# A stack of four graph layers on one core: products of zeros behind each group's sums on TensorE

## What is computed

```python
edge_index = jnp.stack([src, dst])
h = relu(layernorm(x)); x = x + L0(h)   # GAT: scores from 2 vectors, softmax over each target's edges
h = relu(layernorm(x)); x = x + L1(h)   # relational: a row of h @ W[type] for each edge, summed at dst
h = relu(layernorm(x)); x = x + L2(h)   # two GCN convolutions: rows summed at dst, twice
h = relu(layernorm(x)); x = x + L3(h)   # two transformer convolutions, 4 heads, softmax over edges
...
def _transformer_conv(x, src, dst, ea, Wq, bq, Wk, bk, Wv, bv, We, Ws, bs, H, C):
    ...
    alpha = jnp.einsum('ehc,ehc->eh', q[dst], kj) / jnp.sqrt(jnp.asarray(C, x.dtype))
    amax = jax.ops.segment_max(alpha, dst, num_segments=n)
    p = jnp.exp(alpha - amax[dst])
    denom = jax.ops.segment_sum(p, dst, num_segments=n)
    w = p / denom[dst]
    msg = (vj * w[..., None]).reshape(-1, H * C)
    out = jax.ops.segment_sum(msg, dst, num_segments=n)
    return out + x @ Ws + bs
```

## Time and profile before

| | before |
|---|---|
| three runs | 4387.75 us median (4380.13 to 4401.72) |
| profiled execution | 4389.91 us, span 4387.9 us |
| granted TensorE clock, mean | 0.772 |
| busy, share of the span | PE 64%, PEld 46%, DVE 47%, ACT 35%, POOL 54% |
| products (PE) | 15364 |
| DVE's 104 additions, first to last start: L0 | 253.9 to 883.8 us |
| the same: L1 | 985.5 to 1566.9 us |
| the same: L2, first and second | 1649.9 to 2158.3, 2209.9 to 2727.2 us |
| the same: L3, first and second | 2921.3 to 3545.6, 3706.9 to 4347.7 us |

### The profile page before, as it was taken

How to read it: one execution, slowest core, us unless ns; L and a number is a source line. 1 busy time by engine, 2 the same in 40 slices (tenths; PEclk the granted TensorE clock), 3 DMA queues, 4 the chain that set the end, 5 groups by cost and what they waited for, 6 DMA issues and landing times.

```text
span 4387.9 us, 52346 instructions
## 1 busy us (share of the span) xinstructions
PE 2793.6 (64%) x15364; PEld 2036.7 (46%) x15364; DVE 2080.7 (47%) x4427; ACT 1555.9 (35%) x3919; POOL 2371.9 (54%) x2449
## 2 busy tenths in 40 slices
PE   3177788872333356877767877557676774666667
PEld 2055556632222334555534554345555553455555
DVE  5033334641222345566546655235555663555557
ACT  2054444540000033333343333234454423444443
POOL 1745555116666636666366664335666534555653
PEclk9976666885555668899879988567888886887887
DMA  4322222131111112222122221345555424455541
GB/s 86 68 56 59 62 60 62 23 130 47 46 46 48 45 56 53 53 53 53 53 61 55 53 52 34 105 126 141 139 144 146 129 81 128 135 139 135 146 135 45
DMA packets 351656, 360.74 MB, mean 82 GB/s; under 512 B 125198, under 2 KB 274389, under 8 KB 351381
## 3 DMA queue, kind: packets, MB, share of 16 engines
q0 software_dynamic: 89600, 211.77, 18.4%
q1 hardware_dynamic: 255638, 143.69, 12.7%
q10 hardware_dynamic: 6148, 1.93, 0.3%
HBM read 327.08 MB, written 30.26 MB: 81 GB/s over the span
## 4 chain that ended last, share of the span: by engine, by line
PE 41%; another core or an unknown queue 21%; DVE 15%; issue 15%; ACT 3%; POOL 1%; DMA 1%; SPq 1%; DVEq 1%; ACTq 1%; POOLq 0%
PE QX L1368 20%; PE NU L1368 12%; PE MTB L1368 7%; DVE sums_transposed L834 3%; DVE extra_sums_transposed L834 2%; DVE gathered_rows L834 1%; DVE messages L834 1%; DVE query_key_products L834 1%; POOL gathered_rows L549 1%; PE MID L1368 1%; SPq L436 1%; DVE scan_scores L981 1%; ACT window_distance L698 1%; ACTq L601 0%
## 5 line engine op out<-in xcount | busy, mean ns | idle before, releaser
L532 POOL DMA_INDIRECT gathered_rows<-key_value_rows,src_index x832 | 829.6, 997 | 646.2 <-DVE messages L834 356.3
L834 DVE TENSOR_TENSOR sums_transposed<-sums_transposed,NU 128x512 f32 x624 | 425.7, 682 | 1140.7 <-remote 740.6
L549 POOL DMA_INDIRECT gathered_rows<-gcn_rows,src_index x720 | 684.5, 951 | 470.0 <-issue 194.6
L532 POOL DMA_INDIRECT gathered_rows<-gat_rows,src_index x416 | 397.0, 954 | 391.6 <-DVE messages L1008 191.1
L1368 PE MATMUL NU<-start_penalty,zero_weights 128*128 128x512 bf16 x624 | 278.5, 446 | 423.1 <-DVE sums_transposed L834 328.1
L549 POOL DMA_INDIRECT gathered_rows<-relation_rows,src_relation_index x416 | 400.9, 964 | 206.2 <-issue 123.8
L794 ACT ACTIVATE gathered_rows<-iota_window,dst_in_window_by_edge 128x128 f32<-128x128 f32 x832 | 265.1, 389 | 608.4 <-remote 445.0
L729 ACT ACTIVATE edge_node_onehot<-iota_window,dst_in_window_by_edge 128x128 f32<-128x128 f32 x1248 | 394.8, 387 | 155.1 <-remote 135.4
L1368 PEld LDWEIGHTS NU<-edge_node_onehot,messages 128*128 128x128 f32 x2496 | 414.0, 234 | 47.0 <-issue 26.5
L1368 PE MATMUL NU<-gathered_rows 128*128 128x128 f32 x2496 | 395.5, 310 | 56.5 <-issue 33.3
L1368 PE MATMUL NU<-edge_node_onehot,messages 128*128 128x128 f32 x2496 | 413.6, 318 | 24.7 <-issue 24.6
(11 more groups left out here) (294 smaller groups left out, 4357.0 us busy)
## 6 DMA issues: line engine op xcount, KB each, us to landing
query_window<-query_rows SPq DMA_DIRECT2D x832, 66.0 KB
dst_in_window_row<-dst_in_window SPq DMA_DIRECT2D x156, 256.0 KB
gathered_rows<-key_value_rows,src_index POOLq DMA_INDIRECT x832
relation_rows<-gathered_rows SPq DMA_DIRECT2D x25, 512.0 KB
gathered_rows<-gcn_rows,src_index POOLq DMA_INDIRECT x720
dst_in_window_row<-src_place_and_block SPq DMA_DIRECT2D x28, 256.0 KB
gathered_rows<-gat_rows,src_index POOLq DMA_INDIRECT x416
query_window<-gat_target_scores SPq DMA_DIRECT2D x416, 2.0 KB
```

Source lines behind the costliest of these rows:

```text
L532: pool.indirect_dma_start(out=rows_of(a, s)[:, t, :], out_offset=None, in_=a["table"], in_offset=bass.IndirectOffsetOnAxis(ap=srcI[:, TPG ...
L549: pool.indirect_dma_start(out=linear_rows(p["k"], k)[:, t, :], out_offset=None, in_=p["table"], in_offset=bass.IndirectOffsetOnAxis(ap=p[" ...
L834: return dve.tensor_tensor(o, x, y, op)
```

## The change

Behind the sums of a group TensorE now issues the clear of the next group's bank, and ahead of that clear the same product of zeros several times more. Each writes zeros into the bank that is about to be cleared, so nobody reads them. In the attention passes `stay_busy(s)` does it at the end of steps 2 to 114: 14 products in each of the steps 2 to 10, in which no sums run yet, then five and the clear up to step 103, then the clear alone. In `linear` it is 14 and the clear in the relation pass, four and the clear in the GCN passes, and the clear alone behind a pick. In all, 3591 products of zeros are added. The clear of NU leaves `node_sums`, where it had stood behind the wait for the messages; its new wait is for DVE's addition of two groups before (`nu_used`).

```diff
+    FILLING, SUMMING, BETWEEN = 14, 6, (15, 5, 5)
...
+            def keep_busy(bank, n):
+                for _ in range(n):
+                    mm(bank[:, 0:SPAN], zeros_w[:], fpen[:, 0:TPG, :].rearrange("q c p -> q (c p)"))
...
                     pe.wait_ge(S["msg_ready"], b + s + 1)
-                    clear(NU[s % 2], P)
                     for t in range(TPG):
...
+                def stay_busy(s):
+                    g = s + 1 - LAG
+                    if s == 2:
+                        if L3:
+                            pe.wait_ge(S["fin_used"], NBK * (2 + k))
+                        else:
+                            pe.wait_ge(S["idx_ready"], 2)
+                    if g >= 2:
+                        pe.wait_ge(S["nu_used"], b + g - 1)
+                    if g < 0:
+                        keep_busy(NU[g % 2], FILLING)
+                    else:
+                        keep_busy(NU[g % 2], SUMMING - 1 if s < NG else 0)
+                        clear(NU[g % 2], P)
...
+                    if 2 <= s < NG + LAG - 1:
+                        stay_busy(s)
...
-                    if K >= 2:
-                        pe.wait_ge(S["lin_used"], K - 1)
-                    clear(NU[k % 2], P)
+                    if k == 0:
+                        if K:
+                            pe.wait_ge(S["lin_used"], K - 1)
+                        clear(NU[0], P)
...
+                    if k + 1 < NG:
+                        if K:
+                            pe.wait_ge(S["lin_used"], K)
+                        keep_busy(NU[(k + 1) % 2], 0 if (p["k"], k) in PICK_AT else BETWEEN[p["k"]] - 1)
+                        clear(NU[(k + 1) % 2], P)
```

## The result

The changed kernel takes 4520.4 us (median of 4 runs, 4511.4 to 4537.1) against 4383.9 us of the kernel before (4 runs): a ratio of 1.031, 95% interval 1.026 to 1.036. It is slower by 3%. I had forecast 4175 us, faster by 5%, in a range of 3960 to 4400 us. Both the sign and the range were wrong.

A forecast was written before the change was run, and what follows sets the result against it. POOL's gathers were taken as every pass's floor, with TensorE's lower clock and late releases above it. From 4390 us, -71 (first attention), -40 (relation), -52 (GCN) and -52 (last two) gave -215: 4175 us, range 3960 to 4400.

The forecast's parts named there:

- The clock rises: TensorE's granted clock was expected near 1.00 in the attention and GCN passes and over 0.8 in the relation pass.
- Rival 3: First attention pass: the clock stays at the lower level, a group becomes 8.1 us, +186 us, 4432 us in all; 5%.
- First attention pass, -71 us: POOL's gathers bind in place of TensorE, a chunk of eight groups falls from 49.0 to 43.5 us, in 13 chunks.
- late releases: Relation pass: DVE and POOL start up to 11 us after the awaited TensorE sums are recorded; POOL waits 60 us so.
- POOL's 520 us: Attention passes: claimed floor from POOL's four gathers a group, 5.0 us a group for 104 groups.
- Relation pass, -40 us: Two thirds of POOL's 60 us of late releases go; zeros hide under POOL's 5.0 us a group.
- Rival 2: Relation pass: 14 zeros stand in series ahead of each group's sums, +320 us, 4535 us in all; 10%.
- GCN passes, -52 us: Two GCN passes: the higher clock gives 36 us, zeros in groups without a pick cost 10, so -26 us each.
- Last two passes, -52 us: Last two attention passes: clock and zeros nearly cancel, shorter late releases add 1 us a chunk, -26 us each.
- The fillings at nothing: Attention steps 2 to 10: 14 zeros a step cost nothing, or up to 28 us a pass if gathers are ahead.
- Moved clear and its wait, nothing: Clear of NU moved ahead of the spreading and the message wait, with a new `nu_used` wait: no cost in all.
- the floors: All six passes: least time set by POOL's gathers, 520 us, or 450 us in the GCN passes; 530 us claimed above.

The follow-up runs named there:

- no_filling: Changed kernel without the 14 products of zeros in attention steps 2 to 10, against the kernel before: 3614.1 us, ratio 1.0031 (1.002 to 1.005).
- second pair: Kernel before and changed kernel, both run again unchanged in one group: 4379.1 us (7 runs) and 4523.4 us (4 runs), ratio 1.033 (1.030 to 1.036).
- clear_only: Changed kernel without any products of zeros, only the moved clear of NU and its wait, against the kernel before: 3607.9 against 3603.7 us, ratio 1.0005.
- summing_b: Changed kernel with only the five zeros per group of attention steps 11 to 103, against the kernel before: 4514.6 against 4429.3 us, one run each.
- relation_only: Changed kernel with only the relation pass's 14 products of zeros per group, against the kernel before: 3613.6 us, ratio 1.0034 (1.002 to 1.005).
- relation_narrow: Changed kernel with only the relation pass's 14 zeros per group, each of 4 columns instead of 512, against the kernel before: 3609.2 us, ratio 1.000.

## Why the prediction was wrong, point by point

- **The clock rises.** Right in direction. It came as forecast where releases come in time (1.00, 1.00, 0.96 and 0.96 in passes 1, 2, 5 and 6 of no_filling). In the long condition it stops at 0.86 to 0.90 in these passes, where I had "near 1.00" for 1, 5 and 6; TensorE still stands there while a release is late. The sentence that I quoted from the Trainium skill ("TensorE: Matmul & The Clock Gate", Part 1, activity releases the throttle) fits the rise from 0.57 to 0.88 in the relation pass. Read as busy time alone it doesn't fit, 4.00 us busy of 4.00 at 0.50. Rival 3, a first pass that stays at the lower level, didn't happen.
- **First attention pass, -71 us. The step that failed** is "POOL's 8 x 5.0 = 40 us bind in place of TensorE's 8 x 4.39 = 35". Measured was +22 us (+34 in the second pair). TensorE's group wasn't 4.39 us: at a clock of 0.86 it is busy for 532.69 us, 5.2 us a group, where it was 516.95 before. So it doesn't fall under POOL's 5.0, and its products hold as much of the chain as before, 307 and 306 us. Nor did the other part of the chain give way, the late releases that I had not put into this term at all: 183 and 179 us. In the second pair they grew, 146 to 194 us, with TensorE again the same (344 and 339). And POOL's 520 us were no floor for this pass.
- **Relation pass, -40 us.** I put the zeros at nothing (4.3 us a group, under 5.0) and let the late releases shrink by two thirds. It was measured at +26 us, twice. POOL's wait went from 60 to 72 us. In the chain of this pass the unknown part did shrink, from 303 to 221 us (52.1 to 36.3%), and in the second pair from 364 to 208 us; TensorE's part grew from 82 to 255 us and from 72 to 273 us. So the added products do change how the releases come, but a group then takes 5.8 us, and with products of 4 columns too. Rival 2 had the sign and the place. Its condition (a late release runs from the moment at which TensorE has finished) isn't what was seen: its +320 us is off by ten, as its "against" said, and that its total, 4535 us, is near the measured 4520 is chance.
- **GCN passes, -52 us.** +10 and +5 us (+8 and +5), at a clock of 0.94 and 0.93. The 50 us of the lower level that I put "70% on the path" brought nothing back. In the short condition these passes take 434 to 435 us in no_filling, with the zeros and a clock of 0.97 and 0.98, and 435 in clear_only at 0.94: neither the clock nor the zeros count there.
- **Last two passes, -52 us.** +10 and +3 us (+6 and +13), and with the attention steps' zeros alone +19 to +37 (summing_b). The clock's term was over-sized: I had TensorE's busy time fall from 444 to 343 us and the zeros add 102, which is 445; measured was 511 us, at a clock of 0.90. And I reckoned that busy time as time on the path.
- **The fillings at nothing.** The text had "up to 28 us a pass if the gathers are ahead"; 14 to 18 us were seen ahead of the passes (13 to 19 in the second pair), and 12 in the short condition, there made good later.
- **Moved clear and its wait, nothing.** Right (clear_only).
- **A slip.** The passes lie 523 us above the floors (3503 - 2980), not 530. Nothing hangs on it.
- **The range.** It ended at 4400 us and left rivals 2 and 3 outside, with 15%. Among them was one case in which the clock rises and the time grows, and only by series work in the relation pass. No rival had zeros that cost in all passes as much as the clock gives, or more, because late releases keep the clock down and stay themselves. That case was not far: the page had 740.6 us of DVE's waits on "remote" and 21% of the chain on an unknown queue. I took POOL's 60 us of that kind in one pass and wrote them down as the one thing that I couldn't explain. I then let the largest unexplained wait of the trace shrink by my own assumption.

What stays open: why a release of TensorE reaches the other engines late while POOL issues gathers, and why in one condition only; how the long condition's +122 us split between fillings, attention steps and relation pass when they act together; why 14 products of 4 columns change the pattern of the releases there; and what the whole change costs in the short condition. The parts of the chain are the profile's inference, and the ends of products in it are modelled.

## What to carry to other kernels

A clock that rises is worth nothing unless that engine's work is what the pass waits for: before pricing it, find the engine that sets the pace at either level (here POOL in the relation pass, 510 us at 0.50 and 513 to 519 at 1.00). Add up, over all engines, the waits that the profile can't name before pricing anything else (here 740 us ahead of one kind of addition, more than every term of my sum), and give them a range to both sides, never a share that goes away. Cut each trace at its own marks: the window of another run hides a few microseconds of just the kind that is sought. An engine that runs ahead through a deep ring has no floor for a stretch that begins after its head start. Filling an engine's idle time is free only where the same wait would have come anyway, and no version tried here that does the whole work beat the kernel before by more than single runs differ, in either condition.

## What the runs showed of the hardware

- The same program took 3604 to 3608 us on three chips and 4379 to 4429 us on two others. The traces of the second kind have late releases of TensorE's semaphores (740 us of DVE's waits in before), those of the first kind have none. Gathers (947 and 958 ns) and additions (681 and 682 ns) take about the same in both.
- In the relation pass of the long condition the late releases go with the gathers (584 to 170 us without), not with their packets (a third of the DMA share: 584 us), nor with the product that carries the release. Of 39 late ones in before, 23 come while POOL issues without a pause. 14 more products a group, of 512 or of 4 columns, turn them from irregular ones of up to 22 us into mostly regular ones of about 9 us, three groups apart.
- Where nothing else holds POOL, wide products on TensorE go with slightly longer gathers: 947 to 948 ns without them or with 4 columns, 956 to 972 ns with 14 of 512 columns a group.
- Products of zeros, 512 columns wide and 14 a group, go with a granted clock of 1.00 over a whole pass, where it is 0.50 without them (relation_only and clear_only). The same number of products of 4 columns leave it where it was (relation_narrow, short condition):

```profile
763.00:1273.00 510.00, 275.18 (x2313) 235.33 (x2348) 150.09 (x215) 0.00 (x0) 384.29 (x404) 0.50 0.19 53
```
